# From cross attention to the feed-forward: one block in place of four, and output weights split a stage earlier

## The chip, the cores and the metric

The kernel runs on 1 core of one Trainium2 chip. A core has a matrix engine (TensorE, PE in the profile), a vector engine (VectorE, DVE), a scalar engine (ScalarE, ACT), a general engine (GpSimd, POOL) and an engine that only issues transfers (SyncE, SP). They run side by side, each through its own list of instructions in order, and wait for each other by semaphores. The metric is the device time of one execution in microseconds (us). Every trace below is of one profiled execution.

## The reference

Two decoder layers over 16 sequences of 64 tokens: 1024 tokens of 512 features, all in float32. Layer 0 has a BiDAF-like attention over a context of 1601 rows, a causal attention and experts. Layer 1 has cross attention, differential attention with a ReLU feed-forward, and a ternary feed-forward. The change lies in layer 1, from the end of cross attention to the end of the ReLU feed-forward:

```python
# cross attention ends with
x = x + (softmax(q k / sqrt(32), masked) v) @ Wo + bo
# differential attention (heads attend over the heads of one token), then its feed-forward
h = _layernorm(x, ln1_g, ln1_b)
q, k, v = h @ Wq.T * scale, h @ Wk.T, h @ Wv.T
att = softmax(einsum('bnqd,bnkd->bnqk', q, k))             # 32 x 32 for each token
out = einsum(att[first] - lam * att[second], v)
out = _rmsnorm(out) * (1.0 - LAMBDA_INIT)
conn = _layernorm(x) + (out @ Wo.T + bo)                   # the skip is the normed x
h2 = _layernorm(conn, ln2_g, ln2_b)
src3 = relu(h2 @ W1.T + b1) @ W2.T + b2                    # 512 -> 2048 -> 512
x = x + conn + src3
```

## The kernel before, in words

A float32 product is made of three TensorE products of a rounded high part and a low rest (`product`, L66 to L71: L69 high by high, L70, L71). ScalarE makes the high part (`split_hi`, L80), VectorE subtracts it for the low part (`split_lo`, L84). So each operand costs one copy on ScalarE and one subtraction on VectorE before TensorE may use it. A "unit" of work here is 12 such products with 512 columns (4 feature blocks of 128, three products each).

The program is a row of blocks (`nc.Block()`). A block ends when all engines are through with their lists; only then does the next begin. Inside a block the order on each engine is the order of the code, written out by hand. In the stretch at hand the blocks are:

- cross attention (`cross_attention_stage`, names `xa_`, `cl_`): 16 batches in a software pipeline. In a batch `highs(b + 1, j)` on ScalarE and `lows(b + 1, j)` on VectorE split the context of the next batch; in the last batch these places are empty. The value weights' last use is the last batch's value tiles.
- `cross_out_stage` (names `co_`, `con_`): Wo of cross attention is loaded by eight transfers (L1924), split, and eight residual tiles of 128 tokens are made (`residual(t)`, into `co_R`). GpSimd adds the bias bo to x beforehand (L1945). VectorE adds each result to x (L2020) and gathers the norm's sums (L219). `TileNorm` then does the layer norm tile by tile in two groups of four (`invert` L228 to L239, `apply` L253 to L257, `turn` L283 transposes on TensorE, `high` and `low` split). `apply` also writes the plain normed x to `diff_c` (L255), which is the skip. Three projections of 8 tiles each follow: q (kept by ScalarE, L1964), k and v (kept by VectorE, L2038, in a ring of four); every tile is stored to DRAM by SP (L1936, L1939). GpSimd clears `di_K` after the first eight tiles (L1947). `head_weights` (L2026 to L2033) are seven tiny VectorE operations. ScalarE's queue issues the reloads in the heads' layout: queries L1843, 32 transfers of keys L1849, 4 of values L1855.
- `differential_stage` (names `df_`): eight rounds of scores, softmax, transposes and weighted sums; then for each of two halves the RMS norm (`means`, `roots`, spread over partitions by ScalarE L2328 and turned by TensorE L2254, applied by VectorE L2417, the result turned L2263 and split L80, L84).
- `project_stage` "pj5": loads and splits Wo, makes 8 tiles, GpSimd adds bo to `diff_c` (L849), VectorE adds the tiles (L841).
- `norm_stage` "n5": the layer norm of `diff_c`, all eight tiles in each step before the next (L133 to L158), transposes, splits.
- `relu_mlp_stage` (names `ml_`): 8 slices of 256 hidden features. A slice is 4 hidden units of 12 products (into `ml_H`) and 8 output tiles of 6 products (into `ml_O`), 96 products. ScalarE makes the ReLU (L2498), VectorE adds the output to x (L2530). GpSimd adds c and b2 to x while slice 0 runs (L2479, L2481).

After it a ternary feed-forward runs as blocks of its own, untouched.

## Time and profile before

| what | us |
|---|---|
| median of 3 runs (lowest, highest) | 3270.04 (3268.96, 3270.71) |
| the profiled execution's own time | 3272.24 |
| its span | 3270.4 |
| TensorE busy | 2914.9 (89%) |
| VectorE busy | 1644.3 (50%) |
| ScalarE busy | 1142.1 (35%) |
| GpSimd busy | 78.2 (2%) |

The profile gives starts on one axis from the span's start. An engine's row says how long it was idle before and who released it. TensorE has two clocks, 1.2 and 2.4 GHz; the granted clock is shown as a share, 0.50 and 1.00. Before the stretch at hand (from about 2600 us) and behind it (from 3084 us) nothing changes in the code, apart from the eight splits in the last batch of cross attention. A wait of TensorE inside the stretch, or a slow clock in it, is what the change can touch; idle time of the other engines only counts where TensorE waits for them or where a block's end does.

### The profile page before, as it was taken

How to read it: one execution, taken by the hardware profiler on the slowest of the kernel's cores; microseconds unless marked ns; L12 is line 12 of the kernel's file. 1: busy time of each engine (PE TensorE's matmuls, PEld its weight loads, DVE VectorE, ACT ScalarE, POOL GpSimd, SP SyncE). 2: the span in 40 equal slices, each digit the busy share in tenths (PEclk: the TensorE clock that was granted, in tenths of full speed). 3: DMA queues.
4: the chain of work that ended last, by engine and by line, in shares of the span. 5: the costliest groups of instructions: out<-in, count | busy, mean ns of one | idle time of the engine just before them, and what ended most of it. 6: DMA issues, size and time to landing. Idle time of an engine off the chain costs nothing. (4 is left out here: it accounts for less than half of the span.)

```text
span 3270.4 us, 56052 instructions
## 1 busy us (share of the span) xinstructions
PE 2914.9 (89%) x23526; PEld 2298.6 (70%) x23532; DVE 1644.3 (50%) x3399; ACT 1142.1 (35%) x1811; POOL 78.2 (2%) x67
## 2 busy tenths in 40 slices
PE   5998778599997999999999999999999987679755
PEld 3444667488886888888888888888888766558522
DVE  5222432434444555555555555554555465564576
ACT  2221212222223433444333444433444333423384
POOL 0000100100000000000000000000000020120000
PEclk9999899799998999999999999999999987789867
DMA  6886010111103110111110111110111029111200
GB/s 230 299 273 225 26 42 1 36 58 39 58 19 129 36 34 24 44 44 44 31 35 24 44 45 44 31 41 17 44 44 47 1 95 131 35 49 52 109 7 26
DMA packets 169956, 213.67 MB, mean 65 GB/s; under 512 B 51840, under 2 KB 121472, under 8 KB 168848
## 3 DMA queue, kind: packets, MB, share of 16 engines
q1 hardware_dynamic: 148656, 206.40, 20.6%
q10 hardware_dynamic: 21088, 4.20, 0.9%
q8 instruction: 164, 2.69, 0.4%
q14 instruction: 48, 0.39, 0.0%
HBM read 197.97 MB, written 10.49 MB: 64 GB/s over the span
## 5 line engine op out<-in xcount | busy, mean ns | idle before, releaser
L69 PE MATMUL xa_J<-xa_c_hi,xa_wk_hi 128*128 128x402 f32 x1024 | 364.9, 356 | 5.9 <-DVE xa_c_lo L84 5.9
L1532 DVE CUSTOM_DVE_ANT_0 xa_pr<-xa_S,xa_m 128x402 f32<-128x402 f32 x512 | 271.1, 572 | 178.7 <-PE xa_S L1686 178.7
L70 PE MATMUL xa_J<-xa_c_lo,xa_wk_hi 128*128 128x402 f32 x1024 | 354.6, 346 | 0.0
L71 PE MATMUL xa_J<-xa_c_hi,xa_wk_lo 128*128 128x402 f32 x1024 | 354.6, 346 | 0.0
L69 PE MATMUL xa_J<-xa_wv_hi,xa_c_hi 128*128 128x512 f32 (+1 forms) x832 | 335.6, 403 | 0.0
L71 PE MATMUL xa_J<-xa_wv_hi,xa_c_lo 128*128 128x512 f32 (+1 forms) x832 | 327.4, 394 | 0.0
L70 PE MATMUL xa_J<-xa_wv_lo,xa_c_hi 128*128 128x512 f32 (+1 forms) x832 | 327.3, 393 | 0.0
L1429 ACT ACTIVATE xa_kT<-xa_J,cl_bk 128x402 f32<-128x402 f32 x256 | 151.8, 593 | 458.0 <-PE xa_J L71 458.0
L1559 DVE TENSOR_TENSOR cl_v<-xa_J,cl_bv 128x512 f32<-128x512 f32 (+1 forms) x208 | 143.5, 690 | 260.0 <-PE xa_J L71 222.3
L1439 ACT ACTIVATE xa_pr<-xa_pr,xa_nm 128x1608 f32<-128x1608 f32 x128 | 208.6, 1632 | 95.4 <-DVE xa_nm L1548 95.4
L69 PEld LDWEIGHTS xa_J<-xa_c_hi,xa_wk_hi 128*128 128x128 f32 x1024 | 193.1, 189 | 67.5 <-ACT xa_kT L1429 39.6
L84 DVE TENSOR_TENSOR xa_c_lo<-main_x,xa_c_hi 128x402 fp32r<-128x402 f32 (+1 forms) x256 | 131.5, 572 | 140.0 <-ACT xa_c_hi L80 140.0
L70 PEld LDWEIGHTS xa_J<-xa_c_lo,xa_wk_hi 128*128 128x128 f32 x1024 | 193.7, 189 | 0.7
L71 PEld LDWEIGHTS xa_J<-xa_c_hi,xa_wk_lo 128*128 128x128 f32 x1024 | 193.5, 189 | 0.0
L69 PEld LDWEIGHTS xa_J<-xa_wv_hi,xa_c_hi 128*128 128x128 f32 (+1 forms) x832 | 153.5, 185 | 54.6 <-issue 10.1
L71 PEld LDWEIGHTS xa_J<-xa_wv_hi,xa_c_lo 128*128 128x128 f32 (+1 forms) x832 | 153.2, 184 | 40.0
L70 PEld LDWEIGHTS xa_J<-xa_wv_lo,xa_c_hi 128*128 128x128 f32 (+1 forms) x832 | 153.5, 184 | 34.8
L1448 ACT ACTIVATE xa_pT<-xa_T 128x512 f32<-128x512 f32 (+1 forms) x128 | 62.6, 489 | 232.1 <-PE xa_T L1705 228.5
L1567 DVE COPY xa_pT<-xa_S 128x512 f32<-128x512 f32 x128 | 86.9, 689 | 102.9 <-PE xa_S L1705 102.9
L1555 DVE TENSOR_SCALAR xa_pr<-xa_pr,xa_ri 128x1608 f32<-128x1608 f32 x128 | 135.3, 1057 | 4.6
L69 PE MATMUL ex_H<-moe_a_hi,ex_w_hi 128*128 128x512 f32 x320 | 127.4, 398 | 10.9 <-DVE ex_w_lo L84 10.9
L71 PE MATMUL ex_H<-moe_a_hi,ex_w_lo 128*128 128x512 f32 x320 | 127.1, 397 | 0.0
(414 smaller groups left out, 5250.6 us busy)
## 6 DMA issues: line engine op xcount, KB each, us to landing
bs_rows<-in_ctx SPq DMA_DIRECT2D x48, 1024.0 KB, 7.8
main_x<-in_ctx_cols SPq DMA_DIRECT2D x192, 201.0 KB, 2.8
bs_cols<-in_ctx_cols SPq DMA_DIRECT2D x24, 802.0 KB, 9.2
main_x<-in_ctx_cols SPq DMA_DIRECT2D x64, 197.5 KB, 2.6
moe_raw<-in_L_ffn_routed_w SPq DMA_DIRECT2D x24, 512.0 KB, 4.4
diff_raw<-in_L_attn_W SPq DMA_DIRECT2D x16, 512.0 KB, 3.5
bs_cols<-in_ctx_cols SPq DMA_DIRECT2D x8, 796.0 KB, 6.2
bidaf_w_raw<-in_L_xattn_W_qv SPq DMA_DIRECT2D x4, 1024.0 KB, 9.6
```

Source lines behind the costliest of these rows:

```text
L69: pe.matmul(out, w_hi, x_hi, start=first, stop=False)
L70: pe.matmul(out, w_hi, x_lo, start=False, stop=False)
L71: return pe.matmul(out, w_lo, x_hi, start=False, stop=last)
L84: return nc.vector.tensor_tensor(lo, x, hi.bitcast(F32), ALU.subtract)
L1429: nc.scalar.activation(kT[:, s, j % 2, :], J[:, bank(b, ("k", u, j, s)), 0:KG], ACT.Identity, bias=bk_sb[:, 2 * u + s:2 * u + s + 1]).then ...
L1439: nc.scalar.activation(pr[:, r, :], pr[:, r, :], ACT.Exp, bias=nm[:, r:r + 1], accum_out=rs[:, r:r + 1]).then_inc(exp_done, 1)
L1448: nc.scalar.activation(pT[0:r, n0:n1, :], TURNED_IN[i][0:r, 0:(n1 - n0) * 2 * P].rearrange("p (n c) -> p n c", c=2 * P), ACT.Copy).then_in ...
L1532: nc.vector.tensor_tensor_reduce(out=pr[:, r, ks], in0=S[:, r, 0:KG], in1=m[:, ks], scale=1.0, scalar=NEVER, op0=ALU.add, op1=ALU.max, acc ...
L1555: nc.vector.tensor_scalar(pr[:, r, :], pr[:, r, :], ri[:, r:r + 1], None, ALU.mult).then_inc(scaled, 1)
L1559: nc.vector.tensor_tensor(v[0:rows(n), value_slot(b, n), :], J[0:rows(n), bank(b, ("v", n)), :], bv_sb[0:rows(n), :], ALU.add)\
L1567: nc.vector.tensor_copy(pT[:, n0:n1, :], TURNED_IN[i].rearrange("p (n c) -> p n c", c=2 * P)).then_inc(t_dve, 1)
```

## The change

1. Cross attention's last batch takes over Wo: SP loads it to `xa_wo_raw` after the context's last groups; ScalarE splits block j after the key tiles of group j (`high_out`), into the room of `wv_hi`; VectorE subtracts (`low_out`) ahead of the masks of group j, block 3 ahead of the last masks. The parts stay in the place of the value weights and are handed on.
2. `cross_out_stage` has no load and split of Wo. `add(t - 3)` now stands ahead of `low_o(t)`. `apply` no longer writes the skip: eight `norm.keep` follow after `low_w(1)`. SP loads two more rows, bo and b2, and GpSimd adds them to the skip and to x, 16 additions behind its memset of K.
3. `differential_stage`, `project_stage` "pj5", `norm_stage` "n5" and `relu_mlp_stage` become one block. Wo, gamma, beta and the first slices of W1 and W2 are loaded during the last rounds of attention, into the room of the queries; Wo's splits stand beside the last results. The residual tiles go between the norms of the second half; they use the banks T and O in a ring of three. The layer norm is `TileNorm` in two groups. Hidden units of slice 0 stand between the last turns. GpSimd adds c to x (8 additions) after the last low part. Slices 1 to 7 are as before.

```diff
@@ cross_attention_stage, last batch
+                def high_out(k):
+                    if k == 0:
+                        act.wait_ge(wo_loaded, 16 * sum(len(p) for p in pieces))
+                        act.wait_ge(v_made, KT * BATCH)
+                    split_hi(nc, wv_hi[:, k, :], wo_raw[:, k, :]).then_inc(wo_hi_ready, 1)
...
                         if j < 3 and b < LAST:
                             highs(b + 1, j)
+                        if b == LAST:
+                            high_out(j)
...
                         if b < LAST:
                             lows(b + 1, j)
+                        else:
+                            low_out(j)
                         masks(b, 1, j)
+                low_out(KC - 1)
                 last_masks(LAST, 1)
@@ TileNorm
-        if self.kept is not None:
-            v.tensor_scalar(self.kept[:, t, :], x, m, self.rstd[:, 0, t:t + 1], ALU.subtract, ALU.mult)
...
@@ cross_out_stage
-                for k in range(KC):
-                    for p0, row, n in pieces[k]:
-                        sp.dma_start(wo_raw[p0:p0 + n, k, :], Wo[row:row + n, :]).then_inc(wo_loaded[k], 16)
...
                 nc.gpsimd.memset(ins.K[:], 0.0).then_inc(ins.k_cleared, 1)
+                pool.wait_ge(later_loaded, 32)
+                for t in range(TILES):
+                    pool.wait_ge(c_ready, t + 1)
+                    nc.gpsimd.tensor_tensor(c[:, t, :], c[:, t, :], later_rows[:, 0, :], ALU.add)
+                    nc.gpsimd.tensor_tensor(x_sb[:, t, :], x_sb[:, t, :], later_rows[:, 1, :], ALU.add)
...
                 for t in range(3, TILES):
+                    if t < 7:
+                        add(t - 3)
                     low_o(t)
-                    if t - 3 < 4:
-                        add(t - 3)
...
                 low_w(1)
+                for t in range(TILES):
+                    norm.keep(dve, t).then_inc(c_ready, 1)
@@ differential_stage, SP and TensorE behind the rounds
+                sp.wait_ge(scored, WORK)
+                for k in range(KC):
+                    sp.dma_start(wo_raw[:, k, :], Wo[k * P:(k + 1) * P, :]).then_inc(wo_loaded[k], 16)
...
+                sp.wait_ge(wo_lo_ready, KC)
+                sp.dma_start(raw1, w1_slices(W1)[0]).then_inc(w1_loaded, 16)
...
                 mean_squares(LAST)
+                residual(0)
+                residual(1)
                 turn_spread(1)
+                residual(2)
                 turn_result(1)
+                for t in range(3, 6):
+                    residual(t)
+                norm.turn(pe, 0)
+                residual(6)
+                norm.turn(pe, 1)
+                residual(7)
+                norm.turn(pe, 2)
+                norm.turn(pe, 3)
+                pe.wait_ge(w1_lo_ready, 1)
+                pe.wait_ge(added, TILES)
+                pe.wait_ge(norm.lo_ready, 4)
+                hidden_unit(0, 0)
+                norm.turn(pe, 4)
+                hidden_unit(0, 1)
+                for t in range(5, TILES):
+                    norm.turn(pe, t)
+                pe.wait_ge(norm.lo_ready, TILES)
+                hidden_unit(0, 2)
+                hidden_unit(0, 3)
+                pe.wait_ge(w2_lo_ready, 1)
+                for t in range(TILES):
+                    out_tile(0, t)
...
```

What the change does to the order is seen at three places. First VectorE at the start of `cross_out_stage` (`di_K` holds the split attention output, `co_R` the residual tile, `con_` the norm). Before:

```order
L84 TENSOR_TENSOR di_K<-main_qoT,di_K 128x4x128 x3
L84 TENSOR_TENSOR co_w_lo<-di_V,co_w_hi 128x512 x4
L84 TENSOR_TENSOR di_K<-main_qoT,di_K 128x4x128
L2020 TENSOR_TENSOR main_x<-co_R,main_x 128x512
L219 BN_STATS con_stats<-main_x 128x6
L84 TENSOR_TENSOR di_K<-main_qoT,di_K 128x4x128
```

And now:

```order
L84 TENSOR_TENSOR di_K<-main_qoT,di_K 128x4x128 x3
L2051 TENSOR_TENSOR main_x<-co_R,main_x 128x512
L219 BN_STATS con_stats<-main_x 128x6
L84 TENSOR_TENSOR di_K<-main_qoT,di_K 128x4x128
L2051 TENSOR_TENSOR main_x<-co_R,main_x 128x512
```

The four weight splits are gone, and the first addition stands ahead of the fourth low part.

Second, GpSimd at the end of the same stage (`co_later` holds the rows bo and b2). Before:

```order
L1945 TENSOR_TENSOR main_x<-main_x,co_bo 128x512 x8
L1947 MEMSET di_K 128x8192
L1918 UNCONDITIONAL_BRANCH
L843 UNCONDITIONAL_BRANCH
L849 TENSOR_TENSOR diff_c<-diff_c,pj_bias_row 128x512 x8
```

And now (the pair L1982, L1983 stands eight times in all):

```order
L1976 TENSOR_TENSOR main_x<-main_x,co_bo 128x512 x8
L1978 MEMSET di_K 128x8192
L1982 TENSOR_TENSOR diff_c<-diff_c,co_later 128x512
L1983 TENSOR_TENSOR main_x<-main_x,co_later 128x512
L1982 TENSOR_TENSOR diff_c<-diff_c,co_later 128x512
```

The additions of bo to the skip have moved from the projection to the place right behind the memset, and those of b2 with them.

Third, VectorE from the first half's RMS scaling on (`df_T`, `df_O` now hold residual tiles, `dn_` is the norm). Before:

```order
L2417 TENSOR_TENSOR df_o<-df_o,df_S 128x16x32 x4
L84 TENSOR_TENSOR di_K<-df_S,di_K 128x4x4x32 x4
L2395 TENSOR_SCALAR df_ms<-df_M 128x64
L2404 RECIPROCAL df_r<-df_r 128x64
L2406 TENSOR_TENSOR df_r<-df_r 128x64
L2407 TENSOR_TENSOR df_r<-df_r,df_ms 128x64
```

And now:

```order
L2615 TENSOR_TENSOR df_o<-df_o,df_S 128x16x32 x4
L84 TENSOR_TENSOR dm_wo_lo<-main_qoT,dm_wo_hi 128x512 x4
L2593 TENSOR_SCALAR df_ms<-df_M 128x64
L84 TENSOR_TENSOR di_K<-df_S,di_K 128x4x4x32 x4
L2602 RECIPROCAL df_r<-df_r 128x64
```

Further on in the same row, behind the roots, the additions of residual tiles stand ahead of the second half's scaling:

```order
L2623 TENSOR_TENSOR diff_c<-df_T,diff_c 128x512
L219 BN_STATS dn_stats<-diff_c 128x6
L2623 TENSOR_TENSOR diff_c<-df_T,diff_c 128x512
L219 BN_STATS dn_stats<-diff_c 128x6
L2615 TENSOR_TENSOR df_o<-df_o,df_S 128x16x32 x4
L2623 TENSOR_TENSOR diff_c<-df_O,diff_c 128x512
L219 BN_STATS dn_stats<-diff_c 128x6
```

Wo's splits stand ahead of the first half's low parts, and tiles 0 and 1 of the projection are done before the second half is normed.

## Rows read from the trace of the kernel before

**Rows 1.** Windows: us, busy time (count) by engine, TensorE's clock, DMA share, GB/s.

```profile
2651.30:2661.30 10.00, 2.03 (x11) 1.15 (x9) 9.93 (x16) 0.60 (x1) 0.00 (x0) 0.71 0.00 0
2661.30:2731.00 69.70, 69.60 (x304) 57.06 (x304) 31.26 (x56) 13.13 (x21) 6.95 (x1) 0.97 0.58 164
2873.00:2904.50 31.50, 8.14 (x33) 6.17 (x33) 28.06 (x56) 7.19 (x12) 0.00 (x0) 0.57 0.21 51
2928.40:3084.00 155.60, 155.13 (x673) 126.13 (x671) 73.83 (x106) 50.01 (x69) 3.60 (x3) 1.00 0.11 37
```

**Rows 2.** Timeline of TensorE: start, us, instruction, idle before and its releaser.

```profile
2625.67 0.76 PE L69 MATMUL co_R<-co_w_hi,di_K 128*128 128x512 f32 x1 [6.42 <-DVE co_w_lo L84]
...
2832.14 3.67 PE L2254 MATMUL df_S<-main_ident,df_spread 128*128 128x128 f32 x16 [6.05 <-ACT df_spread L2328]
2838.39 1.15 PE L2263 MATMUL df_S<-df_o,main_ident 32*32 32x512 f32 x32 [2.57 <-DVE df_o L2417]
2847.29 0.80 PE L69 MATMUL pj_out<-pj_w_hi,di_K 128*128 128x512 f32 x1 [7.75 <-DVE pj_w_lo L84]
...
2904.47 0.80 PE L69 MATMUL ml_H<-diff_a_hi,ml_w_hi 128*128 128x512 f32 x1 [4.02 <-DVE ml_w_lo L84]
2905.07 0.63 PE L70 MATMUL ml_H<-diff_a_lo,ml_w_hi 128*128 128x512 f32 x1
2905.49 0.63 PE L71 MATMUL ml_H<-diff_a_hi,ml_w_lo 128*128 128x512 f32 x1
...
2928.40 0.39 PE L69 MATMUL ml_H<-diff_a_hi,ml_w_hi 128*128 128x512 f32 x1
```

**Rows 3.** Timeline of VectorE, end of cross attention and start of `cross_out_stage`.

```profile
2601.01 0.58 DVE L1532 CUSTOM_DVE_ANT_0 xa_pr<-xa_S,xa_m 128x402 f32<-128x402 f32 x1 [1.99 <-PE xa_S L1686]
...
2623.02 1.90 DVE L84 TENSOR_TENSOR di_K<-main_qoT,di_K 128x512 fp32r<-128x512 f32 x3 [5.49 <-ACT di_K L80]
...
2633.92 1.71 DVE L84 TENSOR_TENSOR di_K<-main_qoT,di_K 128x512 fp32r<-128x512 f32 x1
```

**Rows 4.** Timeline of VectorE, the norm of `cross_out_stage`.

```profile
2643.43 0.37 DVE L228 BATCH_NORM_AGGREGATE con_mv<-con_stats 128x2 f32<-128x6 f32 x4
...
2645.40 0.75 DVE L253 SCALAR_TENSOR_TENSOR di_V<-main_x,con_mv,co_gamma 128x512 f32<-128x512 f32 x1
2646.07 0.54 DVE L255 TENSOR_SCALAR diff_c<-main_x,con_mv,con_rstd 128x512 f32<-128x512 f32 x1
2646.53 0.74 DVE L257 SCALAR_TENSOR_TENSOR di_V<-di_V,con_rstd,co_beta 128x512 f32<-128x512 f32 x1
2647.19 0.68 DVE L2020 TENSOR_TENSOR main_x<-co_R,main_x 128x512 f32<-128x512 f32 x1
2647.91 0.69 DVE L219 BATCH_NORM_STATS2 con_stats<-main_x 128x6 f32<-128x512 f32 x1
```

**Rows 5.** Timeline of VectorE at the end of `cross_out_stage`.

```profile
2691.68 2.78 DVE L2031 TENSOR_SCALAR di_wm<-co_side,co_lam 128x2 f32<-128x2 f32 x1
...
2698.32 1.28 DVE L2038 TENSOR_SCALAR co_out<-co_R 128x512 f32<-128x512 f32 x2
```

**Rows 6.** Timeline of ScalarE's transfer queue there.

```profile
2704.21 21.67 ACTq L1849 DMA_DIRECT2D di_K<-diff_k  x32
2726.05 9.33 ACTq L1855 DMA_DIRECT2D di_V<-diff_v  x4
```

**Rows 7.** Timeline of GpSimd in `cross_out_stage`.

```profile
2631.26 11.50 POOL L1945 TENSOR_TENSOR main_x<-main_x,co_bo 128x512 f32<-128x512 f32 x8 [1593.17 <-DMA co_bo<-in_L_xattn_bo]
2687.48 6.95 POOL L1947 MEMSET di_K<- 128x8192 f32 x1 [44.72 <-PE co_R L71]
```

**Rows 8.** Timeline of VectorE at the end of `differential_stage`.

```profile
2821.08 2.48 DVE L2417 TENSOR_TENSOR df_o<-df_o,df_S 128x512 f32<-128x512 f32 x4 [3.71 <-PE df_S L2254]
2840.34 2.48 DVE L84 TENSOR_TENSOR di_K<-df_S,di_K 128x512 fp32r<-128x512 f32 x4 [2.01 <-ACT di_K L80]
```

**Rows 9.** Timeline of ScalarE in slice 0 of the feed-forward.

```profile
2909.98 0.63 ACT L80 ACTIVATE ml_h_hi<-ml_h 128x512 fp32r<-128x512 f32 x1
```

More of the change, by code:

```diff
@@ L1794, in cross_layer @@
             project_stage(nc, "pj2", a_hi, a_lo, [(FEATURES, Wq, bq, HEAD**-0.5, qoT)], prefetch=loads.load_first)
-        cross_attention_stage(nc, loads, qoT, ident)
+        return cross_attention_stage(nc, loads, qoT, ident, Wo, [output_rows(g) for g in range(GR)])
 QH, QD = 32, 16
@@ L1876, in double_values, with cross_out_stage @@
             engine.dma_start(self.V[p0 + VH:p0 + 2 * VH, xs, :], self.V[p0:p0 + VH, xs, :]).then_inc(self.v_loaded[r], 16)
-def cross_out_stage(nc, x_sb, c, oT, Wo, bo, pieces, gamma, beta, weights, scales, ins, ident):
+def cross_out_stage(nc, x_sb, c, oT, wo_hi, wo_lo, bo, gamma, beta, weights, scales, later, ins, ident):
     JOBS = len(weights)
@@ L1929, in _ @@
                 ins.load_lambdas(sp)
+                for i in range(2):
+                    sp.dma_start(later_rows[:, i, :], rows_of(later[i], P)).then_inc(later_loaded, 16)
                 for j in range(1, JOBS):
@@ L2188, in _ @@
                 ins.double_values(sp, 1)
+                with nc.allow_non_contiguous_dma(reason="2048 values, once"):
+                    sp.dma_start(b1_sb[:], b1.rearrange("(c p) -> p c", p=P)).then_inc(b1_loaded, 16)
+                sp.wait_ge(scored, WORK)
+                for k in range(KC):
+                    sp.dma_start(wo_raw[:, k, :], Wo[k * P:(k + 1) * P, :]).then_inc(wo_loaded[k], 16)
+                sp.wait_ge(shifted, WORK)
+                sp.dma_start(gamma_row[:], rows_of(gamma, P)).then_inc(affine_loaded, 16)
+                sp.dma_start(beta_row[:], rows_of(beta, P)).then_inc(affine_loaded, 16)
+                sp.wait_ge(wo_lo_ready, KC)
+                sp.dma_start(raw1, w1_slices(W1)[0]).then_inc(w1_loaded, 16)
+                sp.dma_start(raw2, w2_slices(W2)[0]).then_inc(w2_loaded, 16)
+                with sp.Fori(1, SLICES) as n:
+                    sp.wait_ge(w1_lo_ready, n)
+                    sp.dma_start(raw1, w1_slices(W1)[n]).then_inc(w1_loaded, 16)
+                    sp.wait_ge(w2_lo_ready, n)
+                    sp.dma_start(raw2, w2_slices(W2)[n]).then_inc(w2_loaded, 16)
+            @block.gpsimd
+            def _(pool):
+                pool.wait_ge(norm.lo_ready, TILES)
+                for t in range(TILES):
+                    nc.gpsimd.tensor_tensor(x_sb[:, t, :], x_sb[:, t, :], c[:, t, :], ALU.add).then_inc(joined, 1)
             @block.tensor
@@ L2348, in _ @@
                         spread_out(0)
+                act.wait_ge(exp_done, WORK)
+                for k in range(KC):
+                    high_wo(k)
                 keep(LAST)
@@ L2353, in _ @@
                 high(1)
+                norm.root(act, 0)
+                high_w1(0)
+                norm.high(act, 0)
+                norm.high(act, 1)
+                norm.high(act, 2)
+                norm.root(act, 1)
+                norm.high(act, 3)
+                high_w2(0)
+                act.wait_ge(b1_ready, 1)
+                rectify(0, 0)
+                norm.high(act, 4)
+                rectify(0, 1)
+                for t in range(5, TILES):
+                    norm.high(act, t)
+                rectify(0, 2)
+                rectify(0, 3)
+                high_w1(1)
+                with act.Fori(1, SLICES - 1) as n:
+                    mlp_slice(n, True)
+                mlp_slice(SLICES - 1, False)
             @block.vector
@@ new lines, in _ @@
+                add(3)
+                norm.invert(dve, 0)
+                norm.apply(dve, 0)
+                add(4)
+                norm.apply(dve, 1)
+                add(5)
+                norm.low(dve, 0)
+                norm.apply(dve, 2)
+                add(6)
+                norm.low(dve, 1)
+                norm.apply(dve, 3)
+                add(7)
+                low_w1(0)
+                norm.invert(dve, 1)
+                norm.low(dve, 2)
+                norm.low(dve, 3)
@@ new lines, in _ @@
+                norm.apply(dve, 4)
+                norm.apply(dve, 5)
+                dve.wait_ge(b1_loaded, 16)
+                now_bias(0)
+                norm.low(dve, 4)
+                low_h(0, 0)
+                norm.apply(dve, 6)
+                norm.low(dve, 5)
+                low_h(0, 1)
+                norm.apply(dve, 7)
+                norm.low(dve, 6)
+                norm.low(dve, 7)
+                low_w2(0)
+                low_h(0, 2)
+                low_h(0, 3)
+                low_w1(1)
```

329 lines of the change are left out of this document (173 added, 156 removed).

## The prediction

> **What bounds the kernel now.** I read the page first (TensorE busy 89% of the span), then cut the changed stretch into windows, then took TensorE's timeline at every place where a window showed it idle or at a low clock, and last the timelines of VectorE, ScalarE's transfer queue and GpSimd there. In the windows [rows 1] the reader is to see three kinds of stretch. From 2928.40 to 3084 TensorE is busy 155.13 of 155.60 us at clock 1.00: 7 slices at 22.2 us, or 0.231 us for each of 96 products. Nothing else can shorten that, and the change leaves it alone. From 2661.30 to 2731.00 it is busy too. But from 2651.30 to 2661.30 it works 2.03 us of 10 while VectorE works 9.93, and from 2873.00 to 2904.50 it works 8.14 of 31.5 while VectorE works 28.06: there VectorE's layer norm is the bound. TensorE's rows [rows 2] give the other seams: 6.42 us of waiting for Wo's low part before 2625.67, 6.05 for the spread before 2832.14, 7.75 for the projection's weights at 2847.29, 4.02 for the first slice's at 2904.47. Behind each the clock starts low: products stand 0.42 apart (2905.07 to 2905.49), against 0.23 at the full clock. A unit of 12 takes 5.1 us at the low clock and 2.75 at the full one.
>
> **Part 1, the splits in cross attention.** Three of the four fall where VectorE idles between masks. The fourth stands ahead of the last masks, which VectorE began at 2601.01, 1.99 us after its last work [rows 3]. ScalarE's copy takes 0.63 [rows 9] and VectorE's part 0.7, and the copy starts once the last key tile is kept, which the last scores wait for as well, so the split ends about 0.3 us behind 2601.01. Cost 0.3 us; bounds 0 (it hides) and 1.3 (both in full).
>
> **Part 2, the first half of `cross_out_stage`.** VectorE has the first low part done at 2623.7 (2623.02 and a third of 1.90) [rows 3]. TensorE may start at 2623.8 instead of 2625.67: 1.9 earlier. From there to the q projection VectorE sets the pace. GpSimd started its bias additions at 2631.26 [rows 7], behind eight loads of Wo that SP issued before bo's row; with bo first it starts about 5 us earlier, at 2626 (the eight issues and their share of the transfer). Then I lay VectorE's list out anew: the first residual tile is produced at 2629.1 (a unit at the low clock), add and gather 1.33 (0.68 and 0.69, the second overlapping; [rows 4]), a low part 1.7 as long as GpSimd adds (2633.92 took 1.71, the usual is 0.6 to 0.7; [rows 3]), and so on in turn with the tiles: the norm's first step begins at 2640.6 instead of 2643.43 [rows 4], 2.8 earlier. Each `apply` took 1.79 (2645.40 to 2647.19) with the skip's 0.54 in it; two dependent operations alone take 0.75 + 0.03 + 0.66 = 1.44. Four of them before the q weights' low part: 1.4. So TensorE's start of the projections at 2661.3 [rows 1] comes 4.2 earlier, less the 0.3 of part 1: 3.9, taken as 4.0 below with rounding. Bounds: 1.9, if only TensorE's head start is won, and 5.4, if GpSimd delays none of the low parts.
>
> **Part 3, the second half of it: some is given back.** TensorE ends at about 2731 [rows 1], but the block ends with ScalarE's queue: 32 transfers of keys in 21.67 us from 2704.21, then 4 of values to 2735.38 [rows 6]. The keys wait for k's first four tiles to be stored, the fourth of which VectorE keeps at 2699.60 [rows 5]. Ahead of it VectorE has tiny operations, one of which took 2.78 us until GpSimd's memset was over [rows 5, 7], and the v weights' low part, 2.29 us. GpSimd now goes on adding for 16 times 1.44 = 23 us behind the memset [rows 7], so that low part meets it. By the row of 1.71 a two-input operation then loses about 1.0; I take 1.2 for the long one. The eight skips (8 times 0.5, [rows 4]) lie where TensorE is fully busy and VectorE works 31.26 us of 69.70 [rows 1], and cost nothing; without that cover they would cost 4. The queue starts 4.0 - 1.2 = 2.8 earlier. Bounds: 1.0 (three operations lose 1.0 each) and 4.0 (none).
>
> The Trainium skill, page "SBUF — State Buffer", section "Who interferes with whom", says that GpSimd and VectorE share one pair of ports as an exclusive lock, held for the whole instruction, and that a VectorE operation with two SBUF inputs contends with a GpSimd one that reads SBUF. The rows of 1.71 and 2.78 agree. By the rule an operation waits at most one GpSimd addition for each lock it takes; read so, the loss is at most 1.44 for the low part and the sum moves by 0.2.
>
> **Part 4, the four blocks that become one.** I keep the old axis and lay the new order out. VectorE scales the first half to 2823.56 [rows 8], then Wo's four low parts (2.48, as four splits in rows 8), the means, and the first half's low parts, done at 2829.2; ScalarE's copies of Wo (four, some 2.5 us) lie where it waits for the last sums, while VectorE scales. Loads: Wo is asked for when the last scores are made, over 15 us ahead. TensorE: two residual units from 2829.4 to 2834.9 at the full clock, the 16 spread transposes 2.05 (they took 3.67 at the low one; [rows 2]) to 2837.0; VectorE scales in 2.48 to 2839.6 while TensorE makes tile 2; from the start of the last turn to the last low part it was 2838.39 to 2842.82 = 4.4 [rows 2, 8], now from 2839.9 to 2844.5. From here VectorE has no pause: 5 additions with gather (3 to 7) 6.6, two `invert` of 2.1 (1.97 and hand-off; 2643.43 to 2645.40) 4.2, 4 applies 5.8, 4 low parts 2.4, W1's low part 1.2, in all 20.2. First hidden unit at 2864.9; TensorE is through with tile 7 at about 2857 and idles 5 us or more. Next the chain hidden unit 2.75, ReLU and copy 1.3 (twice 0.63; [rows 9]), the copy and low part of tile 4, the unit's low part, apply 6, tile 5, the second unit's low part, apply 7, turn, copy and low part of tile 7: 6.6 for the six short ones and three of 0.65, 2.9 for the applies, 1.8 for hand-offs of 0.2, less what overlaps: 13.6. Third hidden unit at 2878.6. Two units 5.5, eight output tiles 11.2: slice 1 starts at 2895.3. Against 2928.40 [rows 2] that is 33.1 earlier, with a full clock throughout.
>
> The clock will not be full: at 2829.4 TensorE has idled 3 us, at 2864.9 over 5, and before the third unit it has only short transposes for some 9 us. In the old kernel the clock was low behind waits of 6.42, 6.05 and 7.75 us, and the sparse stretch from 2873.00 had a mean of 0.57. What a low start costs: slice 0 took 23.9 us from 2904.47 to 2928.40 where the later ones take 22.2, so 1.7; the projections' window lost 3% of 69.70, 2.1 [rows 1, 2]; a whole unit at the low clock is 2.4. I take three starts at 2.1, so 6.3, and slice 1 begins 26.8 us earlier. The end stays the same: ScalarE, VectorE and GpSimd (8 additions of 1.44, against tiles 1.4 apart that start 5.5 us later) keep up with slice 0, since only operations of VectorE with two SBUF inputs are slowed and none of them is next for TensorE. Bounds: 33.1 (no low start) and 20 (three of 2.4, and 6 us of hand-offs more than counted).
>
> **Sum.** 2.8 + 26.8 = 29.6 us. The profiled execution took 3272.24 (span 3270.4 and 1.8 around it): 3242.6. The median was 2.2 below that execution: 3240.4.
>
> **Rivals.** (a) The clock holds: TensorE's gaps are short enough and 5 or 6 us more are won; 3270.0 - 2.8 - 33.1 = 3234.1. For it: full clock in all dense stretches. Against: every old gap over 5 us ended low. (b) VectorE's run is longer than counted, by hand-offs of 0.2 to 0.4 in a chain of over 40 dependent steps and by more low clock, 8 us: 3248.4. For it: each step of the new order waits for another engine once. Against: the same code ran in `cross_out_stage` with no gaps [rows 4]. (c) The change doesn't do what it says: the merged block still waits for weights or for GpSimd at each old seam, so only the norm's overlap is won, 10 us: 3260. Against: the loads stand far ahead. (d) Slower: TensorE stays at 1.2 GHz into the slices, since nothing in the merged block drives it densely before them. A slice costs 96 times 0.2 = 19 us more; from 1.6 slices on the 29.6 us are gone, with two it is 3240.4 + 38 = 3278. Against it: the old slices had 1.00 from the first dense unit on.
>
> **Chances.** Forecast, within 3237 to 3245: 0.58. (a) 0.15, (b) 0.18, (c) 0.05, (d) 0.02, and 0.02 for no change. The unknown costs span 1.0 to 4.0 and 20 to 33.1, so 3233 to 3249; the range for 8 in 10 is 3234 to 3248. This kernel's measurement can tell about 0.2%, 6.5 us, from no change: faster 0.96, same 0.02, slower 0.02.
>
> **What would show it.** The first product of `cross_out_stage` 1.9 us closer to the stage's start; the q projection 4 us earlier and the block's end by 3; no gap of four blocks; from the second half's low parts to the first hidden unit a VectorE without pause, some 20 us; low clock at three places; slice 1 about 27 us closer to the last scores than before. Wrong it would be if VectorE shows gaps there, if the slices are not 22.2 us, or if ScalarE's queue starts no earlier.

## The result, and the profile after

| | median of the runs | range | ratio to before, 95% interval |
|---|---|---|---|
| before, same chip | 3269.5 us | 3268.37 to 3270.71 | |
| after | 3239.2 us | 3236.01 to 3241.51 | 0.9908 [0.9896, 0.9920] |

30 us were won, 0.92%. The forecast was 3240.4. The profiled execution of the changed kernel took 3239.01, its span is 3237.1, TensorE is busy 90% of it. Two executions do not lie on one axis: the last group of scores of cross attention, ahead of everything that the change can move but the split itself, starts at 2600.07 before and at 2599.03 after. So I count every time from that row, and say "after the scores" for it.

The windows of the changed kernel, of the stretches that answer to [rows 1], and behind them those of the merged block:

```profile
2645.42:2655.42 10.00, 4.67 (x23) 3.29 (x21) 9.83 (x15) 0.89 (x2) 0.00 (x0) 0.78 0.00 0
2655.42:2725.50 70.08, 70.05 (x304) 57.57 (x304) 34.33 (x59) 13.24 (x21) 29.10 (x17) 0.96 0.60 165
2822.60:2832.00 9.40, 9.40 (x34) 7.62 (x35) 3.46 (x9) 1.91 (x1) 0.00 (x0) 0.68 0.11 43
2832.00:2859.90 27.90, 20.97 (x128) 15.83 (x126) 25.52 (x55) 6.65 (x12) 0.00 (x0) 0.93 0.06 20
2859.90:2876.30 16.40, 11.35 (x41) 8.66 (x41) 9.59 (x16) 4.74 (x8) 0.01 (x1) 0.71 0.00 0
2876.30:2895.50 19.20, 18.45 (x73) 14.73 (x74) 11.22 (x11) 3.59 (x5) 11.79 (x8) 0.91 0.18 56
2895.50:3050.30 154.80, 154.80 (x673) 125.75 (x671) 72.83 (x104) 50.05 (x69) 0.00 (x0) 1.00 0.12 37
```

The reader is to see the last line first: the slices are nearly as before, 22.1 us each at clock 1.00 (22.2 in the kernel before, where the second begins at 2928.40 and the third at 2950.60). In 2832.00:2859.90, the stretch that has taken the place of 2873.00:2904.50 in [rows 1], VectorE still works 25.52 of 27.90 us, but TensorE now works 20.97 beside it. The low clock (0.68, 0.71, 0.91 as means) stands in three windows; the 0.93 of a fourth comes from its end alone, where TensorE stands still from 2855.00 to 2859.90 and the granted clock is 0.59, against 1.00 in the 23 us ahead of that.

TensorE's timeline at the seams, which answers to [rows 2]:

```profile
2599.03 0.94 PE L1708 MATMUL xa_S<-xa_kT,main_qoT 32*64 32x402 f32 x16 [0.78 <-ACT xa_kT L1436]
...
2622.76 0.79 PE L69 MATMUL co_R<-xa_wv_hi,di_K 128*128 128x512 f32 x1 [4.51 <-DVE di_K L84]
2655.45 0.80 PE L69 MATMUL co_R<-co_w_hi,co_a_hi 128*128 128x512 f32 x1 [2.40 <-DVE co_w_lo L84]
2727.77 2.02 PE L2283 MATMUL df_S<-di_K,main_qoT 64*32 64x128 f32 x128 [2.10 <-PEq L1950]
2812.32 1.97 PE L2333 MATMUL df_S<-main_ident,df_spread 128*128 128x128 f32 x16
2822.59 0.79 PE L69 MATMUL df_T<-dm_wo_hi,di_K 128*128 128x512 f32 x1 [2.71 <-DVE di_K L84]
2859.93 0.77 PE L69 MATMUL df_T<-di_a_hi,dm_w_hi 128*128 128x512 f32 x1 [4.95 <-DVE di_a_lo L84]
2860.50 0.63 PE L70 MATMUL df_T<-di_a_lo,dm_w_hi 128*128 128x512 f32 x1
2860.93 0.63 PE L71 MATMUL df_T<-di_a_hi,dm_w_lo 128*128 128x512 f32 x1
...
2876.27 0.79 PE L69 MATMUL df_T<-di_a_hi,dm_w_hi 128*128 128x512 f32 x1 [1.41 <-DVE di_a_lo L84]
2895.48 0.39 PE L69 MATMUL df_T<-di_a_hi,dm_w_hi 128*128 128x512 f32 x1
```

They are, in order: the scores from which I count, the first product of `cross_out_stage`, the q projection, the start of differential attention, the first spread's turn, residual(0), hidden units (0,0) and (0,2), slice 1, the second of the eight. Products 0.43 apart (2860.50, 2860.93) show the low clock; a wait stands ahead of each of its three stretches.

### The profile page after: what moved, and what is told of

It reads as the page before. It is cut to its first block and busy times, and to the rows that moved or that the text cites. A ratio compares the mean times of both kernels' runs of the same rounds, so it can differ in the third digit from the quotient of the medians.

```text
span 3237.1 us, 56018 instructions
## 1 busy us (share of the span) xinstructions
PE 2906.5 (90%) x23526; PEld 2292.8 (71%) x23532; DVE 1640.5 (51%) x3397; ACT 1140.8 (35%) x1811; POOL 76.9 (2%) x67
## 5 line engine op out<-in xcount | busy, mean ns | idle before, releaser
L70 PEld LDWEIGHTS xa_J<-xa_wv_lo,xa_c_hi 128*128 128x128 f32 (+1 forms) x832 | 153.4, 184 | 34.9
```

Of the source, the lines that this page charges most:

```text
L70: pe.matmul(out, w_hi, x_lo, start=False, stop=False)
```

## The experiments

Eleven more runs were made. Each column but the last two is a time after the scores, taken from each kernel's own trace in the way of the rows above, and "to slice 1" is the time from the first spread's turn to slice 1, which is what the merged block costs:

| kernel | first product | q projection | attention starts | spread's turn | to slice 1 | ratio to before |
|---|---|---|---|---|---|---|
| before | 25.60 | 61.27 | 135.92 | 218.78 | 109.55 | 1 |
| after | 23.73 | 56.42 | 128.74 | 213.29 | 83.16 | 0.9908 |
| same_again | 23.83 | 56.55 | 132.73 | 216.93 | 83.13 | 0.9898 |
| late_split | 26.02 | 61.39 | 135.77 | 220.01 | 81.25 | 0.9901 |
| bo_first | 27.95 | 61.37 | 136.01 | 217.16 | 81.82 | 0.9910 |
| cross_only | 23.86 | 56.59 | 130.79 | 212.36 | 108.31 | 0.9984 |
| keep_back | 23.79 | 57.82 | 131.63 | 213.45 | 80.97 | 0.9907 |
| adds_late | 23.84 | 56.56 | 130.75 | 213.17 | 81.04 | 0.9895 |
| no_joins | 23.84 | 56.57 | 132.52 | 215.88 | 80.02 | |
| fill | 23.82 | 56.54 | 129.71 | 213.76 | 74.66 | 0.9879 |
| reorder | 23.81 | 56.54 | 130.89 | 212.76 | 72.62 | 0.9881 |
| reorder_fill | 23.81 | 56.53 | 129.48 | 210.44 | 70.90 | 0.9865 |
| early_w1 | 23.80 | 56.52 | 131.87 | 213.49 | 69.23 | 0.9870 |

Six of these kernels (after, same_again, late_split, bo_first, keep_back, adds_late) have the same order and work in the merged block, and even so take 81.0 to 83.2 us to slice 1, 81.9 on average. A part of that scatter is the clock's: at residual(0) 8 to 15 products stood 0.43 us apart, from (0,0) on 7 to 12, from (0,2) on 8 to 14. The four old blocks took 109.6 and 108.3 (before, cross_only). So the merged block is worth 27.0 us by the means, with single pairs from 25.2 to 28.6.

### same_again: what one execution can tell

The changed kernel, nothing edited.

> The changed kernel once more, for the spread of its own stages from one execution to another. Theory (what comes before ScalarE's queue of keys is fixed to 0.2 us, and the queue and attention scatter by some us, so that the 7.2 us by which differential attention began earlier in the first trace were 4.1 won and 3 chance): first product 23.8, q projection 56.5, queue of keys 100.0 us after the last scores, attention's start anywhere from 128.7 to 132.5 and the first spread's turn from 210 to 216; time 3236 to 3242. Rival (the shorter queue belongs to the changed kernel): attention's start again at 128.7 and the time as before.

3235.85 us (3233.86 to 3245.9), 0.9898 [0.9881, 0.9914]. Up to the q projection the two traces agree to 0.13 us. From there they part: attention began at 132.73 and not at 128.74. ScalarE's queue of transfers, of same_again and then of the changed kernel's first trace, shows where:

```profile
2701.69 21.96 ACTq L1875 DMA_DIRECT2D di_K<-diff_k  x32
2723.82 9.92 ACTq L1881 DMA_DIRECT2D di_V<-diff_v  x4
```

```profile
2699.08 20.11 ACTq L1875 DMA_DIRECT2D di_K<-diff_k  x32
2719.36 7.76 ACTq L1881 DMA_DIRECT2D di_V<-diff_v  x4
```

The same 36 transfers took 32.0 us in one execution and 28.0 in the other (31.2 in [rows 6]); attention itself then scatters by 3.5 us as well (from its start to the spread's turn 81.0 to 84.5 us). So of the 7.2 us by which attention began earlier in the first trace, about 2 were chance: over the nine traces with an early split and the kept tiles behind the norm, attention starts at 130.8 on average, over the three of before, late_split and bo_first at 135.9. That is 5.1, and at the spread's turn it is 5.1 again (213.6 and 218.7). The rival falls, but the theory's own ranges were a little narrow: 132.73 and 216.93 lie just above them, 3235.85 just below.

### late_split and bo_first: what the early split is worth, and why

late_split undoes the title's second half:

```
 cross_attention_stage, last batch:
-    high_out(j) / low_out(j)                  # Wo split beside the last key tiles
 cross_out_stage:
+    sync:   eight loads of Wo's pieces, then bo
+    scalar: high_o(0..2), four splits of Wo, high_o(3..7)
+    vector: low_o(0..2), four low parts of Wo, then as after
```

> The changed kernel with the first words of the title undone: cross attention no longer splits its output weights in its last batch; cross_out_stage loads and splits them between the third and the fourth block of its own input, as before. All else as in the changed kernel. Theory (the product waits for the split, TensorE sets the block's end): the first product of cross_out_stage comes 1.9 us later against the last scores of cross attention, the q projection 2 to 3 later, and so does the block's end: 3239.2 + 1.9 = 3241.1. Rival 1 (the block's end hangs on ScalarE's queue of transfers and not on the products): the end moves by under 0.5 us, 3239.5. Rival 2 (the split in cross attention costs there what it saves): cross attention's end comes 1 to 2 us earlier than in the changed kernel, and the time is 3239 to 3240.

3240.17 us (3234.99 to 3245.98), 0.9901 [0.9886, 0.9916]: the time can't tell it from the changed kernel, the trace can. The first product came 2.3 us later (1.9 was expected), but the q projection 5.0 later and not 2 to 3 (61.39 against 56.42), at the place of the old kernel, though the kept tiles stand behind the norm here too. Cross attention ended no earlier; rival 2 falls, and so does rival 1 as far as a trace goes, since attention starts 5 us after the average of the others. In the time the 5 us are not shown: adds_late, on the same chip, has a median 3.0 us lower, and the ranges overlap. More than the wait for a product is at stake. VectorE's and GpSimd's rows of late_split show what:

```profile
2633.84 11.48 POOL L1975 TENSOR_TENSOR main_x<-main_x,co_bo 128x512 f32<-128x512 f32 x8 [1594.30 <-DMA co_bo<-in_L_xattn_bo]
```

```profile
2635.16 0.69 DVE L2055 TENSOR_TENSOR main_x<-co_R,main_x 128x512 f32<-128x512 f32 x1 [3.95 <-POOL main_x L1975]
2635.88 0.69 DVE L219 BATCH_NORM_STATS2 con_stats<-main_x 128x6 f32<-128x512 f32 x1
2636.49 1.71 DVE L84 TENSOR_TENSOR di_K<-main_qoT,di_K 128x512 fp32r<-128x512 f32 x1
```

GpSimd's additions of bo begin 32.1 us after the scores (25.7 in the changed kernel), since bo's row is loaded behind Wo's eight pieces; VectorE's first addition waits 3.95 us for them, and the low parts that follow lie beside them and take 1.71. In the changed kernel the same rows read:

```profile
2624.70 10.97 POOL L1976 TENSOR_TENSOR main_x<-main_x,co_bo 128x512 f32<-128x512 f32 x8 [1587.60 <-DMA co_bo<-in_L_xattn_bo]
```

```profile
2627.95 0.69 DVE L2051 TENSOR_TENSOR main_x<-co_R,main_x 128x512 f32<-128x512 f32 x1 [4.04 <-PE co_R L71]
2628.68 0.69 DVE L219 BATCH_NORM_STATS2 con_stats<-main_x 128x6 f32<-128x512 f32 x1
2629.28 1.01 DVE L84 TENSOR_TENSOR di_K<-main_qoT,di_K 128x512 fp32r<-128x512 f32 x1
...
2638.87 0.37 DVE L228 BATCH_NORM_AGGREGATE con_mv<-con_stats 128x2 f32<-128x6 f32 x4
```

Now the addition waits for its product alone. Would it be enough to load bo first?

```
 cross_out_stage, sync, on late_split:
+    sp.dma_start(bo_row[:], ...)              # ahead of Wo's pieces
     eight loads of Wo's pieces
-    sp.dma_start(bo_row[:], ...)
```

> late_split with the load of the bias row bo ahead of the eight pieces of Wo on SyncE's queue and not behind them. In late_split GpSimd's additions of bo began 32.1 us after the last scores of cross attention, in the changed kernel 25.7. Theory (half of what the early split gains, it gains by freeing the queue ahead of that row): the additions begin near 25 us, the norm's first step comes 2 to 3 us earlier than late_split's (44.8 after the last scores), and the q projection is at 58.5 and not at 61.4, against 56.4 in the changed kernel. Rival (the product's start alone sets it): 61 still; GpSimd's additions then lie beside VectorE's splits of Wo and stretch them by 0.3 to 1.0 each.

3241.92 us (3236.94 to 3243.09), 0.9910 [0.9893, 0.9927]; the q projection at 61.37. The rival came true. GpSimd began 24.6 us after the scores, and met VectorE's low parts of Wo:

```profile
2624.11 11.92 POOL L1975 TENSOR_TENSOR main_x<-main_x,co_bo 128x512 f32<-128x512 f32 x8 [1586.67 <-DMA co_bo<-in_L_xattn_bo]
```

```profile
2625.69 6.67 DVE L84 TENSOR_TENSOR co_w_lo<-di_V,co_w_hi 128x512 fp32r<-128x512 f32 x4 [1.31 <-ACT co_w_hi L80]
2633.50 0.69 DVE L2055 TENSOR_TENSOR main_x<-co_R,main_x 128x512 f32<-128x512 f32 x1 [1.13 <-PE co_R L71]
```

Four low parts took 6.67 us, 0.98 each above 0.69, and the first product came at 27.95. So an early bo helped only where VectorE had no low parts of Wo to make beside it; of the three orders tried, only the early split gives that. The norm's first step (the aggregate) comes 39.8 us after the scores in the changed kernel, 43.4 before, 44.8 in late_split and 44.8 in bo_first. So the early split is worth 5.0 us of norm here. The product accounts for 2.3; the other 2.7 I put down to GpSimd's additions brought forward without meeting Wo's low parts, which is a remainder and was not run by itself. The load moved alone gives nothing. late_split is even 1.4 behind the old kernel at that step: its GpSimd began 0.9 later (32.1 against 31.2), and one low part more, 0.6, stands behind the first addition. The kept tile's 1.3 makes that up until the q projection.

### cross_only: the first half of the change without the second

```
 cross_attention_stage: as after (the early split)
 differential_layer:  as before the change (attention, projection, norm, feed-forward)
 cross_out_stage:     as after, without GpSimd's 16 later additions
```

> Only the first half of the change: the early split, the additions ahead of the low parts and the kept tiles after the norm; the feed-forward and the output projection are the four old blocks, and GpSimd's 16 additions in cross_out_stage are gone. Theory (the block's end came 7.2 us earlier in the changed kernel's trace, of which attention gave 1.7 back): 3269.5 - 5.5 = 3264.0, and a little less without the 16 additions. Rival 1 (the prediction's count: 4.0 won at the q projection and nothing lost to GpSimd's additions): 3265.5. Rival 2 (the 3 us by which ScalarE's queue of 36 transfers was shorter were chance of one execution): the queue takes 31 us again, and the block's end is about 5 earlier, not 7. With 3264 the merged block is worth 3264 - 3239 = 25.

3265.3 us (3263.82 to 3266.21), 0.9984 [0.9975, 0.9993]: 5.3 us under the kernel before on the same chip (3270.57), with an interval of 2.3 to 8.2 that holds the theory's 5.5 and rival 1's 4.0 alike. The trace says more: 4.7 us at the q projection, 5.1 at attention's start. Its queue took 30.2 us, near rival 2's 31, and attention began 5.1 earlier and not 7: rival 2 came true. What is left to the changed kernel, 0.0076 of 3269.5 or 25 us, is the merged block's; its trace, with the old blocks at 108.3, says 25.2 to 27.3 against the six kernels.

### keep_back: the kept tile back in the norm

```
 TileNorm.apply, between the two steps:
+    if self.kept is not None:
+        self.keep(dve, t)
```

> The changed kernel with the kept tile (0.54 us) back between the two steps of each apply of cross_out_stage's norm, as before the change. Theory (VectorE's run sets the q projection, and the first four applies are on it): an apply takes 1.13 + 0.68 + ... = 1.79 us and not 1.46 from its first step to the next addition, and the q projection comes 4 times 0.33 = 1.3 us later after the last scores, 57.8 and not 56.5; so does the start of ScalarE's queue of keys (100.0 to 101.3). Time 3240.5, which its spread does not tell from 3239.2. Rival (the turns wait for TensorE or ScalarE there): the q projection stays at 56.5.

3237.69 us (3237.39 to 3239.31), 0.9907 [0.9891, 0.9924]. The q projection came at 57.82, 1.3 later, as four applies of 1.79 say; the time shows nothing of it, as expected. ScalarE's queue began 0.8 later (100.82), and attention started at 131.63, within the others' scatter.

### adds_late: GpSimd's additions behind the v weights' low part

```
 cross_out_stage, gpsimd, behind the memset:
     pool.wait_ge(later_loaded, 32)
+    pool.wait_ge(w_lo_ready, JOBS)
```

> The changed kernel, but GpSimd's 16 additions in cross_out_stage wait for VectorE's low part of the v weights. Theory: that low part takes 2.29 us again and not 3.12, the keep of the fourth k tile follows its product at once, and the queue of transfers starts 0.7 us earlier; the block's end follows by 0 to 0.7: 3238.5 to 3239.2. By the prediction's step it is 1.2 us: 3238.0. Rival (the block's end hangs on TensorE's last product by now): the queue starts earlier and the end doesn't move, 3239.2.

3237.18 us (3233.8 to 3239.5), 0.9895 [0.988, 0.991]. The low part took 2.29 us again. In the changed kernel it was stretched, and one GpSimd addition with it:

```profile
2690.71 3.12 DVE L84 TENSOR_TENSOR co_w_lo<-co_raw,co_w_hi 128x2048 fp32r<-128x2048 f32 x1 [0.42 <-ACT co_w_hi L80]
2693.76 1.28 DVE L2069 TENSOR_SCALAR co_out<-co_R 128x512 f32<-128x512 f32 x2
```

```profile
2691.64 3.35 POOL L1982 TENSOR_TENSOR diff_c<-diff_c,co_later 128x512 f32<-128x512 f32 x1
2694.95 1.29 POOL L1983 TENSOR_TENSOR main_x<-main_x,co_later 128x512 f32<-128x512 f32 x1
```

But nothing followed that can be seen: attention began at 130.75, at the average of the nine, and the queue at 99.74 against 100.05. That fits the rival; a gain of 0.3 to 0.7 at attention's start could not be told from one trace. In all thirteen traces attention begins 72.3 to 76.2 us behind the q projection, on average 74.3 in the nine and 74.6 in the three, whenever the queue begins: bo_first's queue began 4.3 us later than late_split's (108.71 and 104.37) and ended at the same place. The stage's end is the queue's end, 1.5 us behind TensorE's last product in the changed kernel and 5.3 behind it in same_again. What fixes that end, if its start does not, is open. So is why bo_first's queue began later: the fourth key tile was kept 100.4 after the scores there and 100.5 in late_split, and GpSimd's memset was over at 94.5 and 94.6.

### fill: is the low clock the price of the gaps?

```
+def fill(bank, count):                        # products that nobody reads
+    pe.matmul(bank, wo_hi[:, 0, 0:P], wo_hi[:, 0, :], start=True, stop=True)   # count times
 11 ahead of residual(0), 19 behind turn 3, 11 behind turn 6, 5 behind turn 7
```

> The changed kernel with products on TensorE whose result nobody reads, in the gaps of the merged block: 11 ahead of residual(0), 19 behind the fourth turn, 11 and 5 ahead of the second half's hidden units. Theory (the low clock behind three gaps costs 2.3 to 2.6 us each, and work in the gap keeps the clock): residual(0), hidden unit (0,0) and (0,2) run with products 0.23 apart from their start; slice 1 starts 7 us closer to the first spread's turn: 3232. Rival 1 (the clock falls all the same, or falls while the fillers run): 3239 to 3242. Rival 2 (VectorE's run is the bound and the products won time for nothing): the clock holds, but slice 1 comes only 2 to 3 us earlier, 3236.5.

3231.32 us (3230.52 to 3232.99), 0.9879 [0.9864, 0.9894]. The theory held, and slice 1 came 6.3 to 8.5 us closer to the spread's turn than in the six kernels with the changed kernel's order and work (after, same_again, late_split, bo_first, keep_back, adds_late: 81.0 to 83.2). TensorE's rows of fill at hidden unit (0,0), and its windows at the three places:

```profile
2853.78 0.66 PE L286 MATMUL df_S<-main_ident,main_qoT 128*128 128x128 f32 x4 [1.64 <-DVE main_qoT L255]
2854.19 4.57 PE L2360 MATMUL df_O<-dm_wo_hi 128*128 128x512 f32 x19
2859.38 0.47 PE L69 MATMUL df_T<-di_a_hi,dm_w_hi 128*128 128x512 f32 x1 [0.62 <-DVE di_a_lo L84]
```

```profile
2821.95:2831.00 9.05, 9.00 (x43) 7.11 (x43) 5.71 (x13) 2.81 (x4) 0.00 (x0) 1.00 0.34 118
2859.38:2865.00 5.62, 5.62 (x26) 4.60 (x27) 3.38 (x7) 1.81 (x3) 0.00 (x0) 1.00 0.00 0
2872.40:2878.00 5.60, 5.59 (x24) 4.55 (x25) 1.88 (x2) 1.32 (x2) 5.56 (x4) 1.00 0.28 94
```

The wait of 4.95 us has become one of 0.62 behind 19 filler products, and the clock is 1.00 (2.4 GHz) where it was 0.68 to 0.91. Neither rival fits. The time agrees: adds_late and late_split, on the same chip, are 5.9 and 8.9 us slower.

### reorder: the same instructions in another order

```
 vector:  ... add(7), low(2), low_w1(0), low(3), invert(1), apply(4..7), low(4..7), low_h(0,0), low_h(0,1)
 tensor:  turn(3), hidden(0,0), turn(4), turn(5), hidden(0,1), turn(6), turn(7), hidden(0,2)
 scalar:  high(3) ahead of root(1); high(4..7) ahead of the second ReLU
```

> The changed kernel with another order in the merged block's norm: VectorE takes the low parts of the third and fourth tile before it inverts the second group's variance, and the four applies of the second group stand in one run; TensorE turns tiles 4 and 5 behind hidden unit (0,0), 6 and 7 behind (0,1); ScalarE's high parts follow. No instruction is added or left out. Theory (hidden unit (0,0) waits for VectorE's run, and (0,2) for turns that wait for applies placed too late): (0,0) starts 1.9 us earlier; from (0,0) to (0,2) it takes 11.7 us and not 15.6 to 16.3; with a shorter idle TensorE may keep its clock at (0,2), 2.6 more. Slice 1 comes 6 to 9 us earlier: 3239.2 - 7 = 3232. Rival (the applies in one run delay the first group's hidden units, and what is won at (0,2) is lost at (0,0)): slice 1 within 2 us of the changed kernel's, 3238 to 3241.

3230.26 us (3227.64 to 3231.6), 0.9881 [0.9864, 0.9897]. From hidden unit (0,0) to (0,2) it took 10.7 us (16.3 in the changed kernel, 15.6 in adds_late), and the clock held at (0,2), with only turns and a wait of 1.57 us ahead of it. Slice 1 came 8.4 to 10.5 us closer, a little more than the 6 to 9 expected, and the rival falls:

```profile
2856.76 0.76 PE L69 MATMUL df_T<-di_a_hi,dm_w_hi 128*128 128x512 f32 x1 [3.09 <-DVE di_a_lo L84]
2861.16 1.04 PE L286 MATMUL df_S<-main_ident,main_qoT 128*128 128x128 f32 x8
2864.84 1.03 PE L286 MATMUL df_S<-main_ident,main_qoT 128*128 128x128 f32 x8
2867.45 0.50 PE L69 MATMUL df_T<-di_a_hi,dm_w_hi 128*128 128x512 f32 x1 [1.57 <-DVE di_a_lo L84]
```

### reorder_fill and early_w1: both together, and one thing more

reorder_fill is reorder with 11 filler products ahead of residual(0), 12 behind turn 3 and 5 behind turn 7.

> The kernel reorder with products whose result nobody reads: 11 ahead of residual(0), 12 behind the fourth turn, 5 behind the eighth. Theory (order and clock are two separate costs): the 7 us of the order and, of the fillers' 8 us, the two at residual(0) and at (0,0), some 5: 3239.2 - 7 - 5 = 3227, the fastest. Rival (both take the same time away, since the gaps are the same): no faster than fill alone, 3231.

3224.08 us (3223.38 to 3228.93), 0.9865 [0.9848, 0.9881]: the fastest by its median. In the traces order and clock add up only in part: 8.4 to 10.5 us by the order (72.6 against the six kernels' 81.0 to 83.2; the clock kept at (0,2) is in it), and 1.7 more by the fillers, where the theory wanted 4 to 5. The time says otherwise: reorder's median, on the same chip, is 6.2 us higher, their profiled executions 3.8 apart, of which 2.3 lie ahead of the spread's turn. Whether the fillers are worth 1.7 or more stays open. The rival, no faster than fill, falls.

early_w1 takes two low parts of weights out of VectorE's way (ScalarE's high part of the first goes ahead with it) and has 7 fillers behind turn 3:

```
 vector:  add(0), low_w1(0), add(1), scale(1) ...          # was between low(2) and low(3)
          add_out(0, 0..3), low_w1(1), add_out(0, 4..7)    # was ahead of add_out(0, 0)
```

> reorder_fill with two low parts of weights moved out of VectorE's way: that of the first hidden weights (1.2 us) goes from the norm's run into VectorE's gap between the first two additions of the projection, with ScalarE's high part ahead of it; that of the second slice goes behind the fourth output addition of slice 0. The fillers behind the fourth turn are 7 and not 12. Theory (VectorE's run sets hidden unit (0,0)): it starts 1.2 us closer to the first spread's turn than in reorder_fill (42.6 there), and TensorE's wait of 0.76 in slice 0's output tiles goes: 3224 - 2 = 3222. Rival (the clock was held by the number of fillers, not by their place): with 5 fewer it falls ahead of (0,0), and 2.3 us are lost: 3224 to 3225.

3225.63 us (3224.45 to 3227.94), 0.9870 [0.9853, 0.9886]. In the trace 1.7 us came: 0.6 at (0,0), where from residual(0) on it was the 1.1 that the theory wants and 0.5 had been lost ahead of it, and 1.0 in slice 0, whose wait of 0.76 us is gone (that wait comes and goes without an edit, as no_joins' section shows); 7 fillers held the clock as 12 had. The time does not show it, and the 3222 expected did not come: its attention started 2.4 us later than reorder_fill's, and that is more. Which of the two is faster stays open.

### no_joins: GpSimd's additions beside slice 0

```
 differential_stage, gpsimd:
-    x_sb[:, t] += c[:, t]    # eight tiles; the output lacks the residual
```

> The changed kernel without GpSimd's eight additions of c to x beside slice 0: the output lacks the residual. Theory: VectorE's low parts there take 0.69 and 1.21 us again (1.67, 1.81 and 2.30 in the changed kernel), TensorE's wait of 0.75 us in slice 0's output tiles is gone, and slice 1 comes 0.75 earlier against hidden unit (0,2). Rival: the low parts were not what the output tiles waited for, and nothing moves.

One execution, 3237.77 us. The low parts took 0.69, 0.69 and 1.23 again, the wait is gone, and from (0,2) to slice 1 it took 17.9 us, against 19.2 in the changed kernel. That looks like the theory, but it is not shown. The changed kernel's rows, TensorE's wait and VectorE's low parts ahead of it:

```profile
2889.92 0.47 PE L69 MATMUL df_S<-dm_w_hi,dm_h_hi 128*128 128x512 f32 x1 [0.75 <-DVE main_x L2645]
```

```profile
2885.14 1.81 DVE L84 TENSOR_TENSOR dm_h_lo<-dm_h,dm_h_hi 128x512 fp32r<-128x512 f32 x1 [1.14 <-ACT dm_h_hi L80]
2886.87 2.30 DVE L84 TENSOR_TENSOR dm_w_lo<-main_qoT,dm_w_hi 128x1024 fp32r<-128x1024 f32 x1
```

And VectorE's in bo_first, which has all of GpSimd's additions:

```profile
2889.14 0.69 DVE L84 TENSOR_TENSOR dm_h_lo<-dm_h,dm_h_hi 128x512 fp32r<-128x512 f32 x1 [1.11 <-ACT dm_h_hi L80]
2890.09 1.97 DVE L84 TENSOR_TENSOR dm_w_lo<-main_qoT,dm_w_hi 128x1024 fp32r<-128x1024 f32 x1 [0.26 <-ACT dm_w_hi L80]
```

bo_first has no such wait and took 18.2 us there; late_split, keep_back and adds_late have none either. With the additions in place the wait stood in two of the six traces of this order. So no run ties the 1.3 us to the additions: the wait of 0.75 in it comes and goes with them in place, and bo_first, at 18.2, comes within 0.2 us of this kernel.

## Why the prediction was right

**Part 1.** The splits in cross attention were put at 0.3 us. The last masks began 1.02 us after the scores, against 0.94 in the kernel before; late_split's cross attention ended no earlier. It cost nothing that can be seen; the 0.3 stands for nothing that a run shows.

**Part 2, too small.** The first product was 1.9 earlier, as worked out. The norm's first step was 3.5 earlier against 2.8, the q projection 4.9 against 3.9: the low parts beside GpSimd took 1.01, 1.17 and 1.34 and not the 1.7 of [rows 3]. Why they lost less was not tried. That bo's row no longer stands behind Wo was in the working; late_split and bo_first leave about half of what the early split gives to it, and show that it is tied to the split. The kept tile's 1.4 was measured at 1.3 by keep_back.

**Part 3, wrong.** 1.2 us were to be given back by GpSimd's additions. The collision is there (3.12 us for 2.29), and the queue did begin 4.1 us earlier (100.05 against 104.14) with the q projection 4.9 earlier, where the working had 2.8 and 4.0. But the step that carried the queue's start over to the stage's end is not borne out: bo_first's queue began 4.3 later than late_split's and ended at the same place. The Trainium skill, page "SBUF — State Buffer", section "Who interferes with whom", has the pair as an exclusive lock held for the whole instruction; the traces agree so far as each VectorE low part lost 0.1 to 1.2 us, less than one GpSimd addition (1.3 to 1.5), and the 3.35 us of one addition beside the long low part shows the same from GpSimd's side. The prediction's row of 2.78 is another case, a tiny operation beside a memset, and agrees only with the lock as such. The bare 4.9 arrives at attention (5.1 over the means), where the sum had 2.8.

**Part 4, right, in its parts too.** From the spread's turn to (0,0) the working gave 46.05 us at the full clock and one low start of 2.1; it was 47.61, and 46.1 to 47.6 over the six kernels. From (0,0) to (0,2) it gave 13.7 and one low start; it was 16.3 (14.4 to 16.3). From (0,2) to slice 1, 16.7 and one low start; it was 19.2 (18.2 to 19.4). Slice 1 came 26.4 us closer to the spread's turn in the two traces of the changed kernel, against 26.8, and 27.0 by the means over all. Three low starts were taken at 2.1 each; a unit at the low clock took 5.26 us (2859.93 to 2865.19) where 2.75 is usual, so 2.5. VectorE's run from the second half's low parts to (0,0) took 19.9 us, against 20.2, with pauses under 0.3 us. One reading in it was wrong: GpSimd was said to slow nothing that TensorE needs next in slice 0. The hidden units' low parts took 1.67 and 1.81 us for 0.69 and those of the weights 2.30, and TensorE waited 0.75 us behind them in two of the six traces.

**Sum.** 29.6 was the forecast; 30.3 and 32.4 are the differences of medians of two series, and 5.1 + 27.0 = 32.1 the sum from the traces, to which slices shorter by 0.1 us each add 0.7 that no term of the prediction holds. The mis-sized term is part 3's, 2.8 for 5.1. That the first series lies within 1 us of the forecast is in part luck: the scatter of some 2 us hides the error of this term. Rival (a), the clock holds, was not what happened by itself; fill made it happen, and its 3231 lies 3 us below the 3234 that the rival gave, since part 3 brought 2.3 more and the merged block 34.9 instead of 33.1. Rival (b) is refuted by the sizes of part 4, (c) by the absent seams, (d) by the clock of 1.00 from slice 1 on. What stood against (d), a full clock "from the first dense unit on", was misread: in [rows 2] the old first unit's products stand 0.42 apart.

## What to carry to other kernels

When blocks are merged, count the waits of TensorE that remain and the unit behind each at the low clock (2.5 us here); either order the other engines' work so that the waits shrink, or put products into them whose results nobody reads, which here gave 6.3 to 8.5 us by the products and 8.4 to 10.5 by the order. Before crediting a wait to the thing waited for, look at what else queues behind the same loads: about half of the early split's gain at the norm came with a bias row, though moving that row alone gave nothing. Before crediting a wait's absence to an edit, look whether it is absent in runs without the edit. And take a stage's price from several executions: here one stage of transfers differed by 4 us between two runs of the same kernel.

## What was not expected of the hardware

- Filler products keep the clock: 19 of them in a wait of 5.2 us, or 7 in one of 2.2 (early_w1), and the products behind stood 0.23 apart, from the second or third on. In reorder turns and a wait of 1.57 us left it at 1.00; in the changed kernel it was low behind turns with waits of 0.68, 2.93 and 1.41 us.
- A queue of 36 transfers on one engine took between 26.7 us (bo_first) and 32.0 us (same_again) of issue time with the same transfers in it; in bo_first, the shortest, it had begun later.
- Beside GpSimd's additions a low part of VectorE (two SBUF inputs) lost between 0.1 and 1.2 us, and the long ones no more than the short: four of 0.69 us took 6.67 together, one of 2.29, with the same number of elements, took 3.12. Small instructions so lost more here.
